# Cross-attention K and V products as one-pass three-term sums, scores in two double banks, softmax sums inverted through transfers

## Chip, cores and metric

The kernel runs on one core of a Trainium2 chip. The metric is the device time of one execution in microseconds (us); the figure for the kernel before is the median of three runs.

## The reference

One transformer block for 8 sequences of 256 tokens, 128 channels wide, with a context of 1601 tokens of 96 channels per sequence. All data are float32.

```python
attn_in  = adaln(x, cond, ...);  x = attn(attn_in, attn_in, sa_...) + x     # self: 256 keys
cross_in = adaln(x, cond, ...);  ctx_n = ln(context, ca_lnc_w, ca_lnc_b)
x = attn(cross_in, ctx_n, ca_...) + x                                       # cross: 1601 keys
h = gelu(adaln(x, cond, ...) @ ff_w1 + ff_b1);  x = h @ ff_w2 + ff_b2 + x

def attn(xq, ctx, wq, wkv, wo, bo):        # 16 heads of 64
    q = heads(xq @ wq);  k, v = split(ctx @ wkv)
    q, k = rope(q), rope(k)                # pairs (even, odd) turned by sine and cosine
    a = softmax(q k^T / 8);  return (a v) @ wo + bo
```

## The kernel before

Everything is kept transposed, channels on the partitions. Heads go in pairs of 2 x 64 = 128 rows. A step is one pair of heads of one sequence, so self-attention and cross-attention have 64 steps each. Each engine has an order written out by hand as a string of words (`CROSS` for cross-attention); a word such as `k1+1` is piece 1 of the K work, for the step one ahead, and `p5+-1` is piece 5 of the products with V, of the step behind. The engines run in their own order and meet only at semaphores, so what stands first in an engine's string and waits holds up all behind it. The ramp strings (`RAMP` and `ramp`) do the same for the change from self- to cross-attention, and the last strings for the end, where the feed-forward layer is worked in beside the last steps.

One cross step does this:

- K (`project_k`): four chunks of 512, 512, 512 and 65 keys. Each is a float32 matmul per head (two halves of the array's columns), into bank `PB[0]` or `PB[1]`. VectorE multiplies by the sine (`turn_k`, L1034, to SBUF `turned`); SyncE sends the rows swapped in pairs to `swapped`; VectorE multiplies the bank by the cosine in place (L1040) and adds `swapped` (L1047). ScalarE copies the bank to `KH`, which rounds it to fp32r, the one-pass format (L728), and VectorE writes the rest `KL = bank - KH` (L1055). Each of these VectorE instructions has one tensor in PSUM and one in SBUF.
- V (`project_v`, L1338): 13 tiles of 124 keys in four groups, float32, into the bank `XB`; ScalarE copies them out.
- Maxima (`max_scores`, L1357): one-pass products Q by K for the row maxima, in `MP`; VectorE reduces each (L1069), seven pieces.
- Scores (`scores`, L1376): 13 tiles in seven units, as four one-pass terms KH QH + KL QH + KH QL - maximum, in the one double bank `SP`; ScalarE takes the exponentials (L851), whose units 0 to 6 are called `e0` to `e6`, into four rotating buffers `P`.
- GpSimd adds the exponentials up (L701, L708), folds the sum (L713), and does the last two parts of Q's rotation (L685, L692). All its operands are in SBUF.
- Products with V (L1390) in `OB`, the sum over the keys (`sums`, L1399, 128x256 in `XB`), its reciprocal on VectorE (`invert`, L1080), the scaling (`divide`, L1086), the output product (L1409) and the addition to `xT` (`add`).

The orders of TensorE and VectorE before:

```python
"a4 k1+1 p2+-1 v3+-1 a5 n0 s4+-1 q+1 p3+-1 a6 s5+-1 p4+-1 v0 k2+1 n1 p5+-1 s6+-1 a0+1 v1 n2 s0 "
"a1+1 p6+-1 k3+1 v2 n3 s1 a2+1 sum+-1 k0+2 n4 s2 a3+1 p0 p1 o+-1 s3",
"am4 kc0+1 kt1+1 am5 qt+1 ka0+1 am6 qc+1 kl0+1 nm n0 kc1+1 ka1+1 kt2+1 kc2+1 n1 am0+1 kl1+1 ka2+1 am1+1 "
"kl2+1 kt3+1 am2+1 kc3+1 rc+-1 dv+-1 ka3+1 am3+1 kl3+1 ad+-1 kt0+2",
```

Of the kernel before, what the change touches and what calls it, by code (L numbers as in the profile page):

```python
# [21 lines left out]
SLOTS = 4  # L22

# [42 lines left out]
def block_kernel(nc, xT_in, cT_in, ctx_in, cols_in, cols96_in, ada_in, packs, w1_in, w2_in,  # L66
# [22 lines left out]
    CROSS = Cross("ca", DC, M, 124, 512,  # L89
# [11 lines left out]
    with ExitStack() as ctx:  # L101
# [5 lines left out]


        xT = sb("xT", [D, T])
        ainT = sb("ainT", [D, T])  # L110
        ctxT_all = sb("ctxT_all", [D, CTX])
# [14 lines left out]
        o_w = [sb(f"o_w{i}", [PAIR, D]) for i in range(PAIRS)]  # L126
# [6 lines left out]
        QH, QL = ([sb(f"{name}{i}", [PAIR, N], F32R) for i in range(UNROLL)] for name in ("QH", "QL"))  # L133
        MX = [sb(f"MX{i}", [PAIR, N], F32R) for i in range(2)]
        qturned, qswapped = ([sb(f"{name}{i}", [PAIR, N]) for i in range(2)] for name in ("qturned", "qswapped"))
        share = sb("share", [PAIR, D], F32R)
        Vb = [sb(f"V{i}", [D, len(CROSS.tiles), PAIR]) for i in range(2)]
        PR = [sb(f"P{i}", [D, 2, W]) for i in range(4)]
        psum_acc = sb("psum_acc", [D, 2, W])
        nmx = [sb(f"nmx{i}", [D, 2, 2], F32R) for i in range(2)]  # L140
        mxc = sb("mxc", [D, 2, 2, len(CROSS.chunks)])
        nmxc = [sb(f"nmxc{i}", [D, 2, 2], F32R) for i in range(2)]
        oraw = sb("oraw", [PAIR, N])
        oT = sb("oT", [PAIR, N])
        oraws = [sb(f"oraws{i}", [PAIR, N]) for i in range(2)]
        oTs = [sb(f"oTs{i}", [PAIR, N]) for i in range(PAIRS)]
        csq = [rope[:, i * CW:(i + 1) * CW].rearrange("p (t c) -> p t c", c=DC) for i in range(2)]
        ctree = sb("ctree", [D, 2 * CT, DC // 2])
# [3 lines left out]
        PB = [ctx.enter_context(nc.psum_tensor(f"PB{i}", [D, 512], F32)) for i in range(3)]  # L152
# [4 lines left out]

        SP, MP, KB, XB = S[0], S[1], PB[0:2], PB[2]

# [13 lines left out]
        s_cols = sem("context_columns_loaded")  # L173
        s_rope = sem("rotations_loaded")
        s_set = sem("constants_set")
        s_rows = sem("stack_rows_set")
# [4 lines left out]
        s_w1 = sem("ff_weights_loaded")  # L181
# [33 lines left out]
        class ContextNorm:  # L215

            def __init__(self):
                self.load = [sem(f"ctx_loaded{b}") for b in range(B)]
# [39 lines left out]
        class CrossSteps:  # L258

            def __init__(self, a):  # L260
                n = a.name
                self.w = [sem(f"{n}_weights_loaded{i}") for i in range(UNROLL)]
                self.wo = [sem(f"{n}_wo_loaded{i}") for i in range(UNROLL)]
# [3 lines left out]
                self.qswap = [sem(f"{n}_q_swapped{i}") for i in range(2)]  # L267
# [4 lines left out]
                self.kt = sem(n + "_k_turned")  # L272
                self.kc = sem(n + "_k_cosines")
# [16 lines left out]
                self.sum = sem(n + "_sum")  # L290
                self.inv = sem(n + "_sum_inverse")
# [9 lines left out]
        tree_ = ctree[:, :, :].rearrange("p a b -> p (a b)")  # L301
        LN2 = LayerNorm("ln2", 0, all_chunks[1:], [SP[:, 0], SP[:, 1]], OB, [MP[:, 0], MP[:, 1]],
                        [tree_[:, 0:LNC], tree_[:, LNC:2 * LNC], PR[3][:, 0]], QK)
        LN3 = LayerNorm("ln3", 1, all_chunks[:-1], KB, MP[:, 0, :], KB, [QK[0], QK[1], turned[2]],
# [30 lines left out]
        NM = 2 * NK - 1  # L335

# [17 lines left out]
        def q_free(eng, J):  # L354

            wait(eng, x.s, times(J, NU) - (UNROLL - 1) * NU)
# [27 lines left out]

        def halves(tile):
            return tile.rearrange("p (a n) -> p a n", n=N)
# [4 lines left out]
        def q_bank(J):  # L391

            return MP[:, 0, 0:N] if J == 0 else XB[:, 0:N]
# [37 lines left out]
        RAMP_DVE = {61: "kt0 kc0", 62: "ka0 kt1 kc1 qt0 qc0 kl0", 63: "ka1 kt2 kc2"}  # L431
        RAMP_ACT = {62: "kh0", 63: "qh0 kh1"}
# [42 lines left out]
        def _(sp):  # L475
# [4 lines left out]
            for dst, source in ((condT, cT_in), (ada, ada_in), (cols, cols_in), (ident, ident_in)):  # L480
                sp.dma_start(dst[:], source).then_inc(s_const, 16)
            def self_weights(J, _):
# [9 lines left out]
                for b in (0, 1) if J == 0 else (J,) if 2 <= J < B else ():  # L492
                    sp.dma_start(ctxT_all[:, TOK + b * CW:TOK + (b + 1) * CW], ctx_in[:, b * CW:(b + 1) * CW]
                                 ).then_inc(cx.load[b], 16)

            def self_swap(J, _):
# [4 lines left out]
                if J == B:  # L501
                    sp.dma_start(cols96[:], cols96_in).then_inc(s_cols, 16)
                if J == 2:
                    for pair in range(PAIRS):
                        sp.dma_start(o_w[pair][:, :], packs["sa"][2][pair]).then_inc(z.wo, 16)
                if ROPE <= J < ROPE + 4:
                    lo, hi = ((J - ROPE + i) * M // 2 for i in range(2))
                    sp.wait_ge(cx.tree, tree_end("var", B // 2 - 1, 2))
                    sp.dma_start(rope[:, lo:hi], rope_in[:, lo:hi]).then_inc(s_rope, 16)
# [39 lines left out]
            do = {"q": swap_q, "k": swap_k, "w": cross_weights_of, "wo": cross_out_weights_of}  # L549
            ramp = "w w+1 k0 k1 q k2 k3"  # L550
# [14 lines left out]
        def _(pool):  # L565
# [73 lines left out]
            def self_attention(do):  # L639
# [11 lines left out]

                def context_second(J, _):
# [23 lines left out]
                run_steps(SELF, in_order(SELF.pool, {"l": low_parts, "f": fold, "cc": context_ahead, "cp": context_first,  # L676
                                                     "cq": context_second}))

            def cross_words():

                def rotate_q(J, _):
                    i = J % 2
                    wait(pool, x.qc, times(J, 1) + 1)
                    wait(pool, x.qswap[i], J // 2 * 32 + 32)
                    pool.tensor_tensor(qrotb[i][:, :], qrotb[i][:, :], qswapped[i][:, :], ALU.add  # L685
                                       ).then_inc(x.qa, 1)

                def low_q(J, _):
                    r = J % UNROLL
# [5 lines left out]
                def accumulate(J, c):  # L695
# [26 lines left out]
            run_steps(a_, in_order(a_.pool, do, ahead(*RAMP_POOL[0].values(), *RAMP_POOL[1].values())))  # L722
# [3 lines left out]
        def _(act):  # L726
            def copy(out, in_):
                return act.activation(out, in_, ACT.Copy)  # L728

            def norm(ln, by=""):  # L730

                def square(k):
                    wait(act, ln.centred, k + 1)
                    wait(act, ln.var, k - 1)
                    act.activation(ln.sq[k % 2][:, :], ln.xc[k][:, :], ACT.Square).then_inc(ln.squared, 1)
# [18 lines left out]
            def self_attention(do):  # L754
# [48 lines left out]

                def context_out(J, _):
# [757 lines left out]
```

## Time and profile before

| | |
|---|---|
| median of 3 runs | 1933.77 us (1933.48 to 1937.64) |
| span of the profiled execution, first to last instruction | 1934.6 us |
| its own time outside the span | the profile gives none |
| busy: TensorE, VectorE, ScalarE, GpSimd | 98%, 82%, 49%, 65% |
| mean granted TensorE clock | 0.986 of full speed |

Matmuls are pipelined, so the busy time of one overlaps that of the next; what a group of them costs is read from its start to the start of the next group. A float32 matmul is shown as two records, an fp32r matmul as one. VectorE and GpSimd work one instruction at a time.

### The profile page before, as it was taken

To read this page: it belongs to the slowest core of one execution; us is meant where nothing else is said; L and a number is where in the kernel's file an instruction comes from. 1 tells how busy PE (TensorE), PEld (TensorE's weight loads), DVE (VectorE), ACT (ScalarE), POOL (GpSimd) and SP (SyncE) were. 2 spreads that over 40 slices of the span, in tenths; PEclk is the share of its full clock that TensorE was granted. 3 is DMA by queue.
4 is the path that set the end of the run, shared out by engine and by line. 5 is a ranking of instruction groups with operands and counts; after the bars stand their busy time and mean duration, and the time that the engine had idled before them with its cause. 6 is when DMAs were issued, how large, how long until landed. Compare 5 with 4: busy or idle time off the path is not lost.

```text
span 1934.6 us, 52084 instructions
## 1 busy us (share of the span) xinstructions
PE 1889.5 (98%) x19952; PEld 1289.2 (67%) x19952; DVE 1582.3 (82%) x2316; ACT 945.2 (49%) x1460; POOL 1266.3 (65%) x816
## 2 busy tenths in 40 slices
PE   7999999979999999999999999999999999999999
PEld 5666767745666666666666666666666666666664
DVE  4999999967888888888888888888888888888842
ACT  3555545533545444445554445455444445544444
POOL 4777756415776676677767677776776667667661
PEclk8999999978999999999999999999999999999999
DMA  5332233211111111111111111111111111111100
GB/s 176 117 88 86 81 112 88 73 33 48 53 54 53 55 51 53 59 55 54 54 51 55 52 58 57 51 56 51 55 50 56 57 54 56 51 53 52 53 29 23
DMA packets 147729, 119.07 MB, mean 62 GB/s; under 512 B 63392, under 2 KB 111648, under 8 KB 147488
## 3 DMA queue, kind: packets, MB, share of 16 engines
q1 hardware_dynamic: 110624, 115.46, 17.9%
q10 hardware_dynamic: 36864, 0.28, 1.0%
q8 instruction: 166, 2.72, 0.6%
q14 instruction: 75, 0.61, 0.1%
HBM read 36.71 MB, written 1.05 MB: 20 GB/s over the span
## 4 chain that ended last, share of the span: by engine, by line
PE 87%; POOL 4%; issue 3%; DVE 3%; DMA 1%; ACT 1%; SPq 0%; ACTq 0%; DVEq 0%; POOLq 0%
PE S L1376 24%; PE OB L1390 20%; PE PB L1338 10%; PE PB L1325 10%; PE S L1357 7%; PE PB L1399 2%; PE PB L1310 2%; PE S L1225 2%; PE PB L1409 1%; PE PB L1191 1%; PE OB L1253 1%; PE OB L1236 1%; DMA swapped<-turned 1%; POOL KL L667 1%; POOL psum_acc L674 1%
## 5 line engine op out<-in xcount | busy, mean ns | idle before, releaser
L708 POOL TENSOR_TENSOR psum_acc<-psum_acc,P 124x1024 f32<-124x1024 f32 (+1 forms) x320 | 689.8, 2156 | 216.9 <-ACT P L851 207.4
L851 ACT ACTIVATE P<-S 124x1024 f32<-124x1024 f32 (+1 forms) x448 | 431.3, 963 | 514.6 <-PE S L1376 513.9
L1069 DVE TENSOR_REDUCE mxc<-S 128x2 f32<-128x1024 f32 x384 | 470.0, 1224 | 94.9 <-PE S L1357 88.1
L1390 PE MATMUL OB<-P,V 124*64 124x256 f32 (+1 forms) x3328 | 437.3, 387 | 0.0
L1390 PEld LDWEIGHTS OB<-P,V 124*64 124x64 f32 (+1 forms) x3328 | 221.4, 137 | 188.7 <-issue 104.8
L701 POOL TENSOR_TENSOR psum_acc<-P 124x1024 f32<-124x1024 f32 x64 | 152.0, 2374 | 213.4 <-ACT P L851 213.4
L1376 PE MATMUL S<-QH,KH 64*124 64x256 f32 (+1 forms) x1664 | 271.8, 323 | 5.8 <-ACT P L851 5.8
L728 ACT ACTIVATE V<-PB 124x512 f32<-124x512 f32 (+1 forms) x320 | 157.2, 491 | 206.4 <-PE PB L1338 167.0
L1376 PEld LDWEIGHTS S<-QH,KH 64*124 64x124 f32 (+1 forms) x1664 | 154.0, 181 | 128.5 <-issue 104.7
L1376 PE MATMUL S<-QL,KH 64*124 64x256 f32 (+1 forms) x1664 | 235.2, 278 | 0.0
L1376 PE MATMUL S<-MX,share 64*124 64x256 f32 (+1 forms) x1664 | 235.0, 278 | 0.0
L1376 PE MATMUL S<-QH,KL 64*124 64x256 f32 (+1 forms) x1664 | 234.8, 278 | 0.0
L1338 PE MATMUL PB<-kv_w,ctxT_all 96*64 96x128 f32 (+2 forms) x3328 | 230.4, 276 | 0.4 <-DVE qrot L1024 0.4
L1325 PE MATMUL PB<-ctxT_all,kv_w 96*64 96x512 f32 (+1 forms) x1024 | 222.2, 512 | 0.1
L1338 PEld LDWEIGHTS PB<-kv_w,ctxT_all 96*64 96x64 f32 (+2 forms) x3328 | 187.4, 135 | 37.1 <-issue 17.7
L1034 DVE TENSOR_TENSOR turned<-PB,rope 128x512 f32<-128x512 f32 (+1 forms) x256 | 145.5, 568 | 74.4 <-PE PB L1325 74.4
L1357 PE MATMUL S<-KH,QH 64*128 64x512 f32 (+1 forms) x1024 | 189.5, 387 | 9.2 <-DVE mxc L1069 6.5
L728 ACT ACTIVATE KH<-PB 128x512 fp32r<-128x512 f32 (+1 forms) x256 | 128.6, 502 | 65.5 <-DVE PB L1047 61.9
L1047 DVE TENSOR_TENSOR PB<-PB,swapped 128x512 f32<-128x512 f32 (+1 forms) x256 | 147.8, 577 | 14.2 <-DMA swapped<-turned 11.8
L1376 PEld LDWEIGHTS S<-QH,KL 64*124 64x124 f32 (+1 forms) x1664 | 155.1, 183 | 3.0
L1376 PEld LDWEIGHTS S<-MX,share 64*124 64x124 f32 (+1 forms) x1664 | 155.2, 182 | 0.0
L1376 PEld LDWEIGHTS S<-QL,KH 64*124 64x124 f32 (+1 forms) x1664 | 154.4, 182 | 0.0
(159 smaller groups left out, 2844.8 us busy)
## 6 DMA issues: line engine op xcount, KB each, us to landing
swapped<-turned SPq DMA_DIRECT2D x512, 128.0 KB, 2.1
kv_w<-sa_kv_dram SPq DMA_DIRECT2D x64, 128.0 KB, 2.3
qswapped<-qturned SPq DMA_DIRECT2D x128, 64.0 KB, 1.9
kv_w<-ca_kv_dram SPq DMA_DIRECT2D x64, 96.0 KB, 2.2
ctxT_all<-ctx_dram SPq DMA_DIRECT2D x8, 624.0 KB, 4.4
q_w<-sa_wq_dram SPq DMA_DIRECT2D x64, 64.0 KB, 2.0
q_w<-ca_wq_dram SPq DMA_DIRECT2D x64, 64.0 KB, 2.0
o_w<-ca_wo_dram SPq DMA_DIRECT2D x64, 64.0 KB, 2.0
```

Of the source, the lines that this page charges most:

```text
L701: pool.tensor_tensor(acc, P_of(J, 0)[0:rows], P_of(J, 1)[0:rows], ALU.add).then_inc(x.acc, 2)
L708: pool.tensor_tensor(acc, acc, P_of(J, c)[0:rows, :, 0:w], ALU.add).then_inc(x.acc, 1)
L728: return act.activation(out, in_, ACT.Copy)
L851: act.activation(P_of(J, c)[0:rows, :, 0:w], SP[0:rows, :, 0:w], ACT.Exp, scale=SCALE).then_inc(x.e, 1)
L1034: dve.tensor_tensor(turned[c][:, 0:w], KB[c % 2][:, 0:w], rope[:, M + lo:M + lo + w], ALU.mult).then_inc(x.kt, 1)
L1047: dve.tensor_tensor(KB[c % 2][:, 0:w], KB[c % 2][:, 0:w], swapped[c][:, 0:w], ALU.add).then_inc(x.ka, 1)
L1069: dve.tensor_reduce(mxc[:, t, :, c:c + 1], MP[:, :, 0:w], AX.X, ALU.max).then_inc(x.am, 1)
L1325: ins = pe.matmul(KB[c % 2][half(h), 0:w], kv_w[J % UNROLL][0:DC, half(h)], ctxT_all[0:DC, at:at + w], start=True, stop=True)
L1338: ins = pe.matmul(XB[a:b, k * PAIR:(k + 1) * PAIR], ctxT_all[0:DC, lo + a:lo + b], kv_w[J % UNROLL][0:DC, PAIR:2 * PAIR], start=True, stop ...
L1357: ins = pe.matmul(MP[:, h, at:at + w], QH[J % UNROLL][half(h), t::2], KH[J % 2][half(h), lo:lo + w], start=True, stop=True)
L1376: ins = pe.matmul(SP[0:w, h, k * N:(k + 1) * N], keys[half(h)], queries[half(h), :], start=(n == 0), stop=(n == len(terms) - 1))
L1390: ins = pe.matmul(OB[half(h), 0:N], Vb[J % 2][0:w, t, half(h)], P_of(J, c)[0:w, h, k * N:(k + 1) * N], start=(t == 0), stop=(t == len(a_.t ...
```

## The change

K and V of the cross-attention are computed from operands split in a rounded part and a rest, as three one-pass terms: high by high, high by low, low by high. The context and the weights are split once each, by ScalarE (rounding copy) and GpSimd (rest), in the last self steps, the ramp, and, for later sequences, in the cross steps. K's matmuls take all 128 columns of the array; V's take the weights of two steps (256 columns) as the moving operand, so V is computed for two steps at once, in seven groups of two tiles.

```diff
 def project_k(J, c):
-    for h in range(2):
-        ins = pe.matmul(KB[c % 2][half(h), 0:w], kv_w[J % UNROLL][0:DC, half(h)],
-                        ctxT_all[0:DC, at:at + w], start=True, stop=True)
+    terms = ((1, high), (0, high), (0, low))
+    for n, (part, context) in enumerate(terms):
+        ins = pe.matmul(bank("k", c, J)[:, 0:w + o], wsplit[:, p, part * PAIR:(part + 1) * PAIR], context,
+                        start=(n == 0), stop=(n == len(terms) - 1))
 def project_v(J, k):
...
+        terms = ((low, 2), (high, 2), (high, 3))
+        for n, (context, part) in enumerate(terms):
+            ins = pe.matmul(bank("v", k, J)[0:w, i * 2 * PAIR:(i + 1) * 2 * PAIR], context,
+                            wsplit[:, p:p + 2, part * PAIR:(part + 1) * PAIR], ...)
```

The scores alternate between two double banks, `SP` and `PB`. The K and V products use the same banks in between, or `XB`; `bank_free` waits for the reader of whatever was in the bank last. So K leaves its bank at once: ScalarE copies it to SBUF (`read_k`, word `kq`), SyncE swaps its rows, and all of the rotation and the rest runs from SBUF to SBUF on VectorE:

```diff
+def read_k(J, c):
+    copy(turned[c][:, 0:a_.chunks[c][1]], k_bank(J, c)).then_inc(x.kq, 1)
 def rotate_k(J, c):
-    dve.tensor_tensor(KB[c % 2][:, 0:w], KB[c % 2][:, 0:w], swapped[c][:, 0:w], ALU.add)
+    raw, other = turned[c][:, 0:w], swapped[c][:, 0:w]
+    dve.tensor_tensor(other, other, rope[:, M + lo:M + lo + w], ALU.mult).then_inc(x.kc, 1)
+    dve.tensor_tensor(raw, raw, rope[:, lo:lo + w], ALU.mult).then_inc(x.kc, 1)
+    dve.tensor_tensor(raw, raw, other, ALU.subtract).then_inc(x.ka, 1)
 def low_k(J, c):
-    dve.tensor_tensor(KL[J % 2][:, lo:lo + w], KB[c % 2][:, 0:w], KH[...].bitcast(F32), ALU.subtract)
+    dve.tensor_tensor(KL[J % 2][:, lo:lo + w], turned[c][:, 0:w], KH[...].bitcast(F32), ALU.subtract)
```

The sum over the keys is copied to SBUF by ScalarE (`sc`), gathered as 128x4 by two transfers (`g`), inverted there by VectorE (`ri`), stored to DRAM by two transfers (`i`) and spread over the rows by two more (`b`); `divide` then reads two SBUF tensors:

```diff
 def invert(J, _):
-    dve.reciprocal(XB[:, 0:N], XB[:, 0:N])
+    wait(dve, x.spread, times(J, 96) + 32)
+    dve.reciprocal(stat[:, :, :], stat[:, :, :])
 def divide(J, _):
-    dve.tensor_tensor(oT[:, :], oraw[:, :], XB[:, 0:N], ALU.mult)
+    wait(dve, x.spread, times(J, 96) + 96)
+    dve.tensor_tensor(oT[:, :], oraw[:, :], sums_sb[:, :], ALU.mult)
```

All orders are new. TensorE's puts the scores in three groups (s0 s1, then s2 s3 s4, then s5 s6) and K two to three steps ahead:

```diff
-"a4 k1+1 p2+-1 v3+-1 a5 n0 s4+-1 q+1 p3+-1 a6 s5+-1 p4+-1 v0 k2+1 n1 p5+-1 s6+-1 a0+1 v1 n2 s0 "
-"a1+1 p6+-1 k3+1 v2 n3 s1 a2+1 sum+-1 k0+2 n4 s2 a3+1 p0 p1 o+-1 s3",
+"a2+1 s0 s1 a3+1 p5+-1 p6+-1 q+2 p0 p1 a4+1 s2 a5+1 s3 s4 a6+1 sum+-1 p2 o+-2 n0 p3 k1+2 v0 k2+2 a0+2 s5 s6  "
+"a1+2 p4 k3+2 n1 n2 v1 v2 k0+3 v3",                                                      # TensorE
+"dv+-2 ka3+1 kl1+1 am3+1 qt+2 am4+1 qc+2 am5+1 kl2+1 kl3+1 ka0+2 n0 am6+1 ad+-2 nm+1 ri+-1 kl0+2 am0+2 ka1+2  "
+"am1+2 ka2+2 n1 am2+2",                                                                  # VectorE
+"e0 e1 oe+-1 kh2+1 kh3+1 e2 e3 sc+-1 e4 kh0+2 n0 qh+2 kq1+2 ve0 mr+1 kq2+2 e5 e6 xh ve1 n1 kq3+2 kh1+2 n2  "
+"ve2 kq0+3 wh+5 ve3",                                                                    # ScalarE
+"c5+-1 cf+-1 c6+-1 ql+1 wl+4 xl+-2 c1 c2 qa+2 c3 c4",                                    # GpSimd
+"q+2 wo+-1 k0+2 g+-1 r+5 k1+2 k2+2 i+-1 k3+2 w+5 b+-1 n")                                # SyncE
```

GpSimd's last addition and the sum's matmul work in a buffer of their own (`folded`). Q has three slots for four. The maximum of the short chunk comes fifth of seven. The ramp and the end have new strings too; at the end the output of step 62 and the inverse of step 63 are worked in between the feed-forward products.

## Rows read from the trace of the kernel before

**Rows 1.** The page, busy time of each engine over the span.

```profile
PE 1889.5 (98%) x19952; PEld 1289.2 (67%) x19952; DVE 1582.3 (82%) x2316; ACT 945.2 (49%) x1460; POOL 1266.3 (65%) x816
```

**Rows 2.** Stretches: length, busy PE, PEld, DVE, ACT, POOL, then PEclk, DMA share, GB/s.

```profile
400.00:440.00 40.00, 33.00 (x186) 21.61 (x186) 18.85 (x32) 14.00 (x24) 2.79 (x3) 0.67 0.07 23
...
600.00:1000.00 400.00, 400.00 (x4456) 274.67 (x4452) 338.23 (x513) 198.11 (x300) 278.53 (x160) 1.00 0.17 54
...
1900.00:1935.00 35.00, 30.98 (x90) 13.73 (x90) 7.08 (x10) 15.62 (x24) 1.12 (x1) 0.98 0.08 30
...
1000.19:1022.83 22.64, 22.64 (x254) 15.54 (x252) 19.11 (x30) 11.30 (x17) 15.79 (x10) 1.00 0.18 59
```

**Rows 3.** What TensorE waited for in the whole span: us, times, longest.

```profile
PE S L1357 <- DVE mxc L1069: 6.5, 6, 2.3
PE S L1376 <- ACT P L851: 5.8, 3, 2.8
```

**Rows 4.** Timeline of TensorE, one cross step: start, us, line, records.

```profile
1000.19 0.51 PE L1357 MATMUL S<-KH,QH 64*128 64x512 f32 x2
1000.53 0.28 PE L1376 MATMUL S<-QH,KH 64*124 64x256 f32 x2
1000.65 0.28 PE L1376 MATMUL S<-QH,KL 64*124 64x256 f32 x2
...
1005.30 1.04 PE L1338 MATMUL PB<-kv_w,ctxT_all 96*64 96x128 f32 x16
1006.18 1.03 PE L1325 MATMUL PB<-ctxT_all,kv_w 96*64 96x512 f32 x4
1007.04 1.03 PE L1390 MATMUL OB<-P,V 124*64 124x256 f32 x8
...
1008.90 1.09 PE L1338 MATMUL PB<-kv_w,ctxT_all 96*64 96x128 f32 x16
1009.92 0.38 PE L1376 MATMUL S<-QH,KH 64*124 64x256 f32 x2
1010.14 0.28 PE L1376 MATMUL S<-QH,KL 64*124 64x256 f32 x2
1010.26 0.28 PE L1376 MATMUL S<-QL,KH 64*124 64x256 f32 x2
...
1014.72 1.03 PE L1325 MATMUL PB<-ctxT_all,kv_w 96*64 96x512 f32 x4
1015.68 0.38 PE L1376 MATMUL S<-QH,KH 64*124 64x256 f32 x2
```

**Rows 5.** Groups by line and shape: busy us, mean ns, idle before.

```profile
L1069 DVE TENSOR_REDUCE mxc<-S 128x2 f32<-128x1024 f32 x384 | 470.0, 1224 | 94.9 <-PE S L1357 88.1
L1034 DVE TENSOR_TENSOR turned<-PB,rope 128x512 f32<-128x512 f32 x192 | 131.6, 685 | 74.4 <-PE PB L1325 74.4
L1034 DVE TENSOR_TENSOR turned<-PB,rope 128x65 f32<-128x65 f32 x64 | 13.9, 217 | 0.0
L1080 DVE RECIPROCAL PB<-PB 128x256 f32<-128x256 f32 x64 | 112.4, 1756 | 12.3 <-PE PB L1399 12.3
L928 DVE RECIPROCAL lnrstd<-lnsd 128x4 f32<-128x4 f32 x3 | 0.5, 175 | 4.7 <-ACT lnsd L740 4.7
L1086 DVE TENSOR_TENSOR oT<-oraw,PB 128x256 f32<-128x256 f32 x64 | 26.9, 421 | 2.2
L708 POOL TENSOR_TENSOR psum_acc<-psum_acc,P 124x1024 f32<-124x1024 f32 x256 | 607.4, 2373 | 207.5 <-ACT P L851 207.1
L851 ACT ACTIVATE P<-S 124x1024 f32<-124x1024 f32 x384 | 393.1, 1024 | 427.7 <-PE S L1376 426.9 <-POOL psum_acc L708 0.5
L728 ACT ACTIVATE KH<-PB 128x512 fp32r<-128x512 f32 x192 | 114.1, 594 | 48.8 <-DVE PB L1047 48.5
```

**Rows 6.** DMA issues: KB each, median us from issue to landing.

```profile
swapped<-turned SPq DMA_DIRECT2D x512, 128.0 KB, 2.1
MX<-nmxc ACTq DMA_DIRECT2D x128, 1.0 KB, 2.0
```

More of the change, by code:

```diff
@@ L22 @@
 SLOTS = 4
+QSLOTS = 3
+LOADS = 2
+TOP = 229344
 class Stage:
@@ L217, in __init__ @@
             def __init__(self):
-                self.load = [sem(f"ctx_loaded{b}") for b in range(B)]
+                self.load = [sem(f"ctx_loaded{i}") for i in range(LOADS)]
                 self.tree = sem("ctx_tree")
@@ L262, in __init__ @@
                 self.w = [sem(f"{n}_weights_loaded{i}") for i in range(UNROLL)]
+                self.raw = [sem(f"{n}_kv_weights_loaded{i}") for i in range(UNROLL)]
+                self.wh = sem(n + "_kv_weights_high")
+                self.wl = sem(n + "_kv_weights_low")
+                self.xh = sem(n + "_context_high")
+                self.xl = sem(n + "_context_low")
                 self.wo = [sem(f"{n}_wo_loaded{i}") for i in range(UNROLL)]
@@ L266, in __init__ @@
                 self.qc = sem(n + "_q_cosines")
-                self.qswap = [sem(f"{n}_q_swapped{i}") for i in range(2)]
+                self.qswap = sem(n + "_q_swapped")
                 self.qa = sem(n + "_q_rotated")
@@ L290, in __init__ @@
                 self.sum = sem(n + "_sum")
+                self.sc = sem(n + "_sum_read")
+                self.spread = sem(n + "_sums_gathered_inverses_spread")
                 self.inv = sem(n + "_sum_inverse")
@@ L728, in copy, with high_weights, high_context @@
                 return act.activation(out, in_, ACT.Copy)
+            def high_weights(p, _):
+                if p < PAIRS:
+                    act.wait_ge(x.raw[p % UNROLL], p // UNROLL * 16 + 16)
+                    if p >= PAIRS // 2:
+                        wait(act, z.y, STEPS // 2)
+                    copy(split_of(p, 0), both_parts(raw_weights(p))).then_inc(x.wh, 1)
+            def high_context(b, k):
+                lo, w = a_.chunks[k]
+                act.wait_ge(cx.done, b * CG + k + 1)
+                if b > 1:
+                    wait(act, x.kp, (b - 1) * PAIRS * NK)
+                    wait(act, x.vp, (b - 1) * PAIRS // 2 * NU)
+                copy(ctxH[b % 2][:, lo:lo + w], ctxT_all[0:DC, b * M + lo:b * M + lo + w]).then_inc(x.xh, 1)
             def norm(ln, by=""):
@@ new lines, in project_k, with project_v @@
+                    terms = ((1, high), (0, high), (0, low))
+                    for n, (part, context) in enumerate(terms):
+                        ins = pe.matmul(bank("k", c, J)[:, 0:w + o], wsplit[:, p, part * PAIR:(part + 1) * PAIR], context,
+                                        start=(n == 0), stop=(n == len(terms) - 1))
+                    ins.then_inc(x.kp, 1)
+                def project_v(J, k):
+                    if v_group(J, k) is None:
+                        return
+                    m, g, n = v_group(J, k)
+                    b, p = batch(2 * m), 2 * m % PAIRS
+                    wait(pe, x.wl, min(2 * m + 1, PAIRS - 1) + 1)
+                    wait(pe, x.xl, b * NK + (sum(a_.tiles[a_.units[g][-1]]) - 1) // a_.chunks[0][1] + 1)
+                    bank_free("v", k, J)
+                    if J == -1:
+                        pe.wait_ge(LN2.unit, NLN - 1)
+                    for i, t in enumerate(a_.units[g]):
+                        lo, w = a_.tiles[t]
+                        high, low = ctxH[b % 2][:, lo:lo + w], ctxL[:, b * M + lo:b * M + lo + w]
+                        terms = ((low, 2), (high, 2), (high, 3))
+                        for n, (context, part) in enumerate(terms):
+                            ins = pe.matmul(bank("v", k, J)[0:w, i * 2 * PAIR:(i + 1) * 2 * PAIR], context,
+                                            wsplit[:, p:p + 2, part * PAIR:(part + 1) * PAIR],
+                                            start=(n == 0), stop=(n == len(terms) - 1))
@@ L1351, in max_scores @@
                         wait(pe, x.qc, 1)
-                    if u == 0 and J == 1:
-                        wait(pe, LN2.unit, NLN - 1)
-                    for t in range(2) if last else (u % 2,):
+                    for t in range(2) if last else (tile,):
                         for h in range(2):
                             at = t * N if last else 0
-                            ins = pe.matmul(MP[:, h, at:at + w], QH[J % UNROLL][half(h), t::2],
+                            ins = pe.matmul(MP[:, h, at:at + w], QH[J % QSLOTS][half(h), t::2],
                                             KH[J % 2][half(h), lo:lo + w], start=True, stop=True)
@@ L1375, in scores @@
                             for h in range(2):
-                                ins = pe.matmul(SP[0:w, h, k * N:(k + 1) * N], keys[half(h)], queries[half(h), :],
+                                ins = pe.matmul(slot(J, c)[0:w, h, k * N:(k + 1) * N], keys[half(h)], queries[half(h), :],
                                                 start=(n == 0), stop=(n == len(terms) - 1))
@@ L1406, in output @@
                     wait(pe, x.ot, times(J, 1) + 1)
-                    x_free(uses, readers, J, ("o", 0))
+                    bank_free("o", 0, J)
                     for h in range(2):
-                        ins = pe.matmul(XB[half(h), 0:N], o_w[r][:, half(h)], oT[:, :], start=True, stop=True)
+                        ins = pe.matmul(bank("o", 0, J)[half(h), 0:N], o_w[r][:, half(h)], oT[:, :], start=True, stop=True)
                     ins.then_inc(x.y, 1)
```

433 lines of the change are left out of this document (271 added, 162 removed), and 10 rows, old and new, of tables (CROSS, SELF).

## The prediction

> **What bounds the kernel now.** First the busy shares of the page: TensorE 98% [rows 1]. Then the stretches: in the cross steps, from 457 to about 1860 us, TensorE is busy all the time at the full clock, and one step of it, from one K/Q maximum group to its repeat, takes 22.64 us [rows 2]. In that step VectorE works 19.11 us, GpSimd 15.79 and ScalarE 11.30 [rows 2]. Then the waits: in the whole span TensorE waits some 6 us each for maxima and exponentials [rows 3]. So 62 of the 64 cross steps, about 1404 us, are TensorE's instruction stream and nothing else. A change is worth what it takes from this stream, as long as no other engine or chain becomes longer than the shorter step.
>
> **K and V products.** Read from start to start, a V group of four tiles takes 0.88 and 1.02 us, a K chunk of 512 keys 0.86 and 0.96 us [rows 4]. K has 1601/512 = 3.13 such chunks: 3.13 x 0.91 = 2.85 us a step. V has 13/4 = 3.25 such groups: 3.25 x 0.95 = 3.09. Together 5.94 us.
>
> After: a pair of one-pass matmuls of 256 columns, which lie on different rows of the array and run together, takes 0.12 us (1010.14 to 1010.26) [rows 4]. A K chunk is three matmuls of 512 columns on all the rows, 3 x 0.23 = 0.70 us plus a start of some 0.06, so 3.13 x 0.76 = 2.4 us a step. V is 39 matmuls of 256 columns in two steps, 19.5 a step, at 0.12: 2.35 us, with three to four starts 2.5. Together 4.9 us: a gain of 1.05 us a step. No row shows a one-pass matmul on 96 rows with 124 or 128 columns of weights. The bounds: nearly the rate of two rows-halves without any overhead, 0.107 us per 256 columns (0.12 less the 0.01 that the spacing may hold), gives 4.4 us and a gain of 1.5; a weight load that doesn't hide, at most the 0.28 us that one matmul record lasts [rows 4], would give 5.5 us for V alone and a loss of 2. I take 0.12, since in the scores two loads and two matmuls fit in that time.
>
> **Order of the score groups.** A score unit that follows a float32 group begins slowly: the second pair starts 0.22 us after the first (1009.92 to 1010.14), against 0.12 after a maximum group (1000.53 to 1000.65) [rows 4]. In the order before six of the seven units follow a float32 group. In the new one all seven follow a maximum group or another unit. That is 6 x 0.10 = 0.6 us a step. Bounds: 0 if the cost returns at other borders, 0.9 if the float32 groups gain at theirs. I take 0.5. The rest of TensorE's stream (13 tiles of scores and of products, maxima, Q, sum, output) is the same.
>
> **TensorE's step after**: 22.64 - 1.05 - 0.5 = 21.1 us.
>
> **VectorE.** The reciprocal falls from 1.76 to 0.18 us [rows 5]. Sine, cosine, join and rest keep their count, three of 512 and one of 65 columns each, at 0.69 and 0.22 us with one tensor in PSUM [rows 5]. So the step falls from 19.11 to 17.5 us, against 21.1: 3.6 us of slack. With both tensors in SBUF the instruction may be somewhat shorter or, if it has to share something, longer; this is the first rival. The reductions pace the maxima: 1.22 us [rows 5] plus a group of 0.34 [rows 4]; the new order has at least 1.4 us of scores between a long pair of them, except behind a4, which is now the short one.
>
> **ScalarE** gets the copies out of the K banks, 3 x 0.59 plus 0.2, the copy of the sum, 0.4, and V in pieces of 256 columns: 11.30 + 2.0 + 0.4 + 0.5 = 14.2 of 21.1 us. Busy time is no limit, its order may be: behind `mr+1`, which waits for the maximum of the next step, stand `kq2`, `e5` and `e6`, and for these TensorE's `k3`, `p4` and `s0`. From a6 to the end of s5 and s6 lie some 6.5 us of TensorE's work; `am6`, `ad` and `nm` need 1.9 of it. Hidden, and it costs up to 1 us a step if VectorE comes late by more than 3 us.
>
> **GpSimd** gets one more subtraction of context per two steps and, in all, eight of weights: 16 to 16.5 us of 21.1. The split of the first context falls in the last self steps, where GpSimd is idle, and ScalarE at half load: 0, at most 3 us.
>
> **Transfers.** The inverse takes three transfers one after another, 2.0 us each [rows 6], plus ScalarE's copy 0.4, and SyncE's queue. `sum` starts some 11 us into the step, the gather lands 3 us later; VectorE comes to `ri` about 2 us after a6, so it may stand 1 us there. SyncE waits at `b` for the store; behind it is only the next Q swap. The spread rows land 11 to 12 us after `sum`, and `dv+-2` is due at about 11.6. So VectorE stalls 1 to 2 us a step, out of 3.6 of slack. I take 0 to 0.2 us a step on TensorE for all new waits, +6 us in all; up to 1.5 a step if the slack is gone.
>
> **Ramp and end.** In the ramp TensorE has half clock for long (0.67 over 40 us) [rows 2]; the new string does more K and V before the first scores and fewer waits between: 0, bounds -15 and +20. At the end, `o0` waits for three transfers (7.5 us) with five feed-forward products, 4.3 us, in between: +3.
>
> **Sum**, against the span of 1934.6 us: 62 x (1.05 + 0.5) = -96, waits +6, end +3: 1847.6, and with the median 0.8 us below the span, 1847 us.
>
> **Rivals.** *First, the other side: VectorE and GpSimd get in each other's way at SBUF's read side.* Before, every large VectorE instruction had one tensor in PSUM, and GpSimd's ran beside it at a constant 2.37 us [rows 5]; no row shows a large VectorE instruction with two SBUF tensors, so none shows whether it can. After, 17 a step have two: 12 x 0.69 + 4 x 0.22 + 0.42 = 9.6 us [rows 5]. GpSimd reads two SBUF tensors in all its 15.8 us [rows 2]. If the two can't run at once, the step is at least 9.6 + 15.8 = 25.4 us; with the durations less their fixed part (0.15 us each for 27 instructions, from the 65- and 512-column forms) 21.4. In between, at 24 to 25, the decision falls to waits: in-order queues lose some again. It decides once the sum exceeds 21.1. 24.5 us gives 62 x 1.9 = +115, about 2050; the bounds are 1870 and 2140. For it: every VectorE form before avoids two SBUF tensors, and 9.6 + 15.8 is over the step. Against it: nothing in the trace, but if the ports share word by word only the lower end remains.
>
> The Trainium skill (SBUF — State Buffer, Who interferes with whom) states that a VectorE instruction with two SBUF inputs contends with a GpSimd instruction that reads SBUF, and that the one that comes second blocks until the first is done. By this rule the upper end holds, 25.4 us a step or more and about 2110 us. No row here can show it.
>
> *Second, new waits eat most of the gain.* The chains through `mr`, `ri` and `dv` and the banks shared by K, V and scores leave the step between 21.7 and 22.8 us. For it: the slack behind nm and dv is 1 to 3 us by the sums above, and a TensorE that idles can lose its clock, as in the ramp [rows 2]. Against it: VectorE's 17.5 us. 22.2 gives 62 x 0.45 = -28, with the end 1909; from 1880 to 1950.
>
> **Chances.** Forecast (1815 to 1880) 0.44; first rival 0.33; second 0.23, of which 0.13 is faster, 0.04 the same and 0.06 slower. A time within 0.2% (1930 to 1938) counts as the same, about what a measurement of this kernel can tell. Faster 0.57, same 0.04, slower 0.39. The range runs from 1810 to 2090: 0.03 lies below and half of the first rival above. The likeliest case's own range is 1815 to 1880.
>
> **What would show it.** A step of 21 us in TensorE's timeline with K chunks at 0.70 to 0.76 us and V groups of six matmuls at 0.72 to 0.8, second score pairs at 0.12 throughout: the forecast. GpSimd's 1024-column additions still at 2.37 us and VectorE's 512-column forms at 0.69 or less: the first rival is wrong; additions of 3 us, or VectorE forms of 1 to 3 us, and TensorE waiting for maxima or exponentials: it is right. Waits of TensorE for `P` with both engines' durations unchanged: the second. My forecast is wrong if the step is above 21.7 us.

## The result, and the profile after

The changed kernel takes 2563.81 us (median of 4 runs, 2557.99 to 2566.91) against 1934.62 us (4 runs): a ratio of 1.325, 95% interval 1.3225 to 1.3276. Slower by a third; the prediction was 1847 and its range ended at 2090. The profiled execution has a span of 2557.8 us. In the fences, the page's busy times, as in [rows 1]; then stretches with the columns of [rows 2], the third of them one cross step between two of Q's matmuls.

```profile
PE 2002.2 (78%) x17616; PEld 1449.0 (57%) x17616; DVE 2195.7 (86%) x2316; ACT 1072.2 (42%) x2011; POOL 1423.5 (56%) x856
```

```profile
400.00:440.00 40.00, 29.52 (x122) 22.17 (x121) 20.39 (x34) 15.06 (x32) 0.98 (x2) 0.63 0.06 21
600.00:1000.00 400.00, 302.11 (x2639) 222.82 (x2640) 355.07 (x360) 161.50 (x315) 221.57 (x116) 0.86 0.13 39
1499.99:1532.62 32.63, 24.52 (x215) 17.68 (x213) 28.83 (x30) 12.68 (x25) 17.70 (x10) 0.84 0.13 39
```

This step went from 22.64 to 32.6 us. The mean of the cross steps, read from one combination of the row maxima (VectorE's `nm`, one a step) to the next, is 32.45 us, and 62 x 9.8 = 608 is nearly the whole loss of 623 between the spans. TensorE no longer fills the step; VectorE does, with 28.8 us in the same 30 instructions, where the forecast had 17.5. Next, the groups of instructions by line and shape (columns of [rows 5]), VectorE's and GpSimd's:

```profile
L1219 DVE TENSOR_TENSOR turned<-turned,rope 128x512 f32<-128x512 f32 x192 | 334.5, 1742 | 0.0
L1218 DVE TENSOR_TENSOR swapped<-swapped,rope 128x512 f32<-128x512 f32 x192 | 322.1, 1678 | 7.5 <-DMA swapped<-turned 7.3
L1228 DVE TENSOR_TENSOR KL<-turned,KH 128x512 fp32r<-128x512 f32 x192 | 252.6, 1316 | 10.6 <-ACT KH L867 10.2 <-issue 0.2
L1221 DVE TENSOR_TENSOR turned<-turned,swapped 128x512 f32<-128x512 f32 x192 | 207.3, 1080 | 6.6
L1259 DVE TENSOR_TENSOR oraws<-oraws,qturned 128x256 f32<-128x256 f32 x64 | 138.3, 2161 | 52.8 <-DMA qturned<-inverses_dram 52.4
L1242 DVE TENSOR_REDUCE mxc<-S 128x2 f32<-128x1024 f32 x384 | 468.6, 1220 | 148.1 <-PE S L1555 147.9
...
L840 POOL TENSOR_TENSOR psum_acc<-psum_acc,P 124x1024 f32<-124x1024 f32 x256 | 634.6, 2479 | 840.6 <-ACT P L1028 831.1
L850 POOL TENSOR_TENSOR folded<-psum_acc 124x512 f32<-124x512 f32 x64 | 103.2, 1612 | 5.0
L827 POOL TENSOR_TENSOR QL<-qrot,QH 128x256 fp32r<-128x256 f32 x64 | 74.8, 1168 | 1.1 <-ACT QH L867 1.1
```

Every 512-column VectorE form with two SBUF tensors has grown, from 0.69 to 1.1 to 1.7 us, and the division from 0.42 to 2.16; the reduction from PSUM keeps its 1.22 [rows 5]. Of the 65-column forms only the rest has grown (0.22 to 0.79). GpSimd's long additions pay less, 2.48 for 2.37 us; its short instructions pay more: the fold 1.61 for 1.28, the rest of Q 1.17 for 0.73. The timelines of both engines (start, us, line) show how:

```profile
1502.44 2.87 DVE L1218 TENSOR_TENSOR swapped<-swapped,rope 128x512 f32<-128x512 f32 x1
1505.23 2.82 DVE L1219 TENSOR_TENSOR turned<-turned,rope 128x512 f32<-128x512 f32 x1
1508.09 0.69 DVE L1221 TENSOR_TENSOR turned<-turned,swapped 128x512 f32<-128x512 f32 x1
1508.70 1.22 DVE L1242 TENSOR_REDUCE mxc<-S 128x2 f32<-128x1024 f32 x1
1509.83 0.41 DVE L1127 TENSOR_TENSOR xT<-xT,XB 128x256 f32<-128x256 f32 x1
```

```profile
1502.40 5.11 POOL L840 TENSOR_TENSOR psum_acc<-psum_acc,P 124x1024 f32<-124x1024 f32 x2
```

GpSimd's first addition starts 0.04 us before VectorE's, which then lasts one addition and its own 0.6; the second does the same, and ends 0.55 us (one short instruction) after GpSimd's pair, at 1508.05 against 1507.51. Once GpSimd stands still, the next form takes 0.69. What TensorE pays for it, in its timeline and in the waits of the whole span (us, times, longest; compare [rows 3]; the first of these is ScalarE's, whose copy of K to `KH` TensorE's maxima need):

```profile
1510.39 1.19 PE L1517 MATMUL XB<-ctxH,wsplit 96*128 96x512 f32 x2 [5.98 <-DVE xT L1127]
```

```profile
ACT KH L867 <- DVE turned L1221: 412.4, 68, 6.8
...
PE XB L1517 <- DVE xT L1127: 300.3, 52, 6.0
...
PE S L1555 <- DVE mxc L1242: 89.2, 71, 5.1
...
PE OB L1588 <- ACT oraws L867: 57.1, 59, 1.9
```

The K product of chunk 2 needs `XB`, which `ad` (L1127) must have read; `ad` stands in VectorE's order behind `kl2 kl3 ka0`, five instructions with two SBUF tensors.

### The profile page after: what moved, and what is told of

Read it like the earlier page. It is cut to its first block, busy times and chain, and to the rows that moved or that the text cites. A ratio compares the mean times of both kernels' runs of the same rounds, so it can differ in the third digit from the quotient of the medians.

```text
span 2557.8 us, 48174 instructions
## 1 busy us (share of the span) xinstructions
PE 2002.2 (78%) x17616; PEld 1449.0 (57%) x17616; DVE 2195.7 (86%) x2316; ACT 1072.2 (42%) x2011; POOL 1423.5 (56%) x856
## 4 chain that ended last, share of the span: by engine, by line
DVE 38%; PE 35%; issue 9%; DMA 8%; SPq 5%; ACT 3%; POOL 2%; ACTq 0%; DVEq 0%; POOLq 0%
DVE KL L1228 8%; DVE turned L1219 8%; PE OB L1588 8%; DVE swapped L1218 8%; DMA qturned<-inverses_dram 5%; DVE oraws L1259 5%; PE XB L1517 4%; DVE mxc L1242 4%; PE S L1555 4%; PE S L1574 4%; PE PB L1574 4%; SPq L633 2%; DMA swapped<-turned 2%; PE S L1399 1%; DVE turned L1221 1%
## 5 line engine op out<-in xcount | busy, mean ns | idle before, releaser
L840 POOL TENSOR_TENSOR psum_acc<-psum_acc,P 124x1024 f32<-124x1024 f32 x256 | 634.6, 2479 | 840.6 <-ACT P L1028 831.1
L1517 PE MATMUL XB<-ctxH,wsplit 96*128 96x512 f32 x248 | 98.2, 487 | 348.7 <-DVE xT L1127 300.3
L1219 DVE TENSOR_TENSOR turned<-turned,rope 128x512 f32<-128x512 f32 (+1 forms) x256 | 348.3, 1360 | 0.0
L1218 DVE TENSOR_TENSOR swapped<-swapped,rope 128x512 f32<-128x512 f32 (+1 forms) x256 | 335.9, 1312 | 8.4 <-DMA swapped<-turned 8.2
L1588 PE MATMUL OB<-P,V 124*64 124x256 f32 (+1 forms) x2236 | 298.8, 400 | 39.5 <-ACT oraws L867 39.4
L1228 DVE TENSOR_TENSOR KL<-turned,KH 128x512 fp32r<-128x512 f32 (+1 forms) x256 | 298.5, 1185 | 10.6 <-ACT KH L867 10.2
L1028 ACT ACTIVATE P<-PB 124x1024 f32<-124x1024 f32 (+1 forms) x224 | 215.7, 963 | 182.2 <-PE PB L1574 176.2
L1028 ACT ACTIVATE P<-S 124x1024 f32<-124x1024 f32 (+1 forms) x224 | 215.8, 963 | 176.6 <-PE S L1574 174.4
L1221 DVE TENSOR_TENSOR turned<-turned,swapped 128x512 f32<-128x512 f32 (+1 forms) x256 | 221.9, 867 | 8.8
L1259 DVE TENSOR_TENSOR oraws<-oraws,qturned 128x256 f32<-128x256 f32 x64 | 138.3, 2161 | 52.8 <-DMA qturned<-inverses_dram 52.4
L1574 PE MATMUL PB<-QH,KH 64*124 64x256 f32 (+1 forms) x832 | 142.4, 328 | 7.9 <-DMA MX<-nmxc 3.2
```

Source lines behind the costliest of these rows:

```text
L1028: act.activation(P_of(J, c)[0:rows, :, 0:w], slot(J, c)[0:rows, :, 0:w], ACT.Exp, scale=SCALE).then_inc(x.e, 1)
L1218: dve.tensor_tensor(other, other, rope[:, M + lo:M + lo + w], ALU.mult).then_inc(x.kc, 1)
L1219: dve.tensor_tensor(raw, raw, rope[:, lo:lo + w], ALU.mult).then_inc(x.kc, 1)
L1221: dve.tensor_tensor(raw, raw, other, ALU.subtract).then_inc(x.ka, 1)
L1228: dve.tensor_tensor(KL[J % 2][:, lo:lo + w], turned[c][:, 0:w], KH[J % 2][:, lo:lo + w].bitcast(F32), ALU.subtract).then_inc(x.kl, 1)
L1259: dve.tensor_tensor(oT[:, :], oraw[:, :], sums_sb[:, :], ALU.mult).then_inc(x.ot, 1)
```

## The experiments

Theory: the two engines exclude each other at SBUF, whole instruction by whole instruction, and VectorE's in-order queue turns that into TensorE's waits. Rivals: the new waits themselves (transfers, banks, orders), or slower one-pass products.

**Take GpSimd's load away (a1, a4).** L1218 to L1259 are as in the change.

```diff
-acc = psum_acc[0:rows, :, 0:w];  ... P_of(J, c)[0:rows, :, 0:w]
+acc = psum_acc[0:rows, :, 0:8];  ... P_of(J, c)[0:rows, :, 0:8]        # a4: 0:256
```

> The changed kernel with GpSimd's additions of the exponentials cut to 8 of their columns (the sums are left wrong; every instruction, wait and order stays). Theory A, VectorE's instructions with two SBUF tensors and GpSimd's block each other: the 512-column K instructions of VectorE fall from means of 1.1 to 1.7 us to 0.7, the step from 32.6 to 21 to 22 us, the time to 1840 to 1920 us. Theory B, the step is long through the new chains of waits (transfers of the inverse, shared banks, in-order queues) and VectorE's durations are long for another reason, such as ScalarE's and the DMAs' traffic in SBUF: durations stay over 1 us and the time over 2400 us.

> The changed kernel with GpSimd's additions cut to half of their columns (256 of 512 per head; the sums are left wrong), 1.28 us each for 2.37. Theory A: what VectorE is held up falls about by half, the step to 26 to 28 us, the time to 2150 to 2300 us. Theory B: over 2400 us.

a1: 2055.69 us (1.0631 [1.06, 1.0662]); a4: 2263.62 (1.1706 [1.1672, 1.174]). With additions of 0.35, 1.39 and 2.48 us the time is 2056, 2264 and 2564: some 200 and 275 us per microsecond of one. Where TensorE or the transfers set the time, it would not follow an engine that idles over 40% of it. a4 is as expected; a1 lies 136 us above the 1840 to 1920 expected. It still has the folds, at 1.60 us, and Q's rest, at 1.17; VectorE's 512-column K forms take 0.71 to 0.97 us in it, so some contention is left, and a2 shows a second cause.

**Take VectorE's second tensor away (a2).** K's rotation, its rest and the division read one SBUF tensor each, through a reduction over groups of one element; the rotation, the rest and the scaling are left out, GpSimd does all its work.

```diff
-dve.tensor_tensor(other, other, rope[:, M + lo:M + lo + w], ALU.mult)
+dve.tensor_reduce(other, other.rearrange("p (n a) -> p n a", a=1), AX.X, ALU.max)
```

> The changed kernel with VectorE's SBUF-to-SBUF instructions of K and the scaling by the inverse replaced by instructions of the same width with one SBUF tensor (a reduction over an axis of length 1; rotation, rest and scaling are left out). GpSimd keeps all its additions. Theory A: about 0.6 to 0.7 us each, GpSimd's additions at 2.37 us, the time 1840 to 1920 us. Theory B, or GpSimd's additions being late by themselves: over 2300 us.

2003.09 us (1.0359 [1.03, 1.0418]). Its groups:

```profile
L1213 DVE TENSOR_REDUCE turned<-turned 128x512 f32<-128x512 f32 x192 | 129.8, 676 | 0.0
...
L840 POOL TENSOR_TENSOR psum_acc<-psum_acc,P 124x1024 f32<-124x1024 f32 x256 | 609.8, 2382 | 361.5 <-ACT P L1028 344.7 <-DMA qswapped<-qturned 7.0
```

Same count, same bytes written, same GpSimd, and both engines are back at their durations of before. 561 of the 623 us are gone. But 2003 is above the 1840 to 1920 expected, and the kernel is still slower than before: its steps take 23.47 us in the mean, against 22.64 before and the forecast's 21.1. So there is a second cause.

**Two SBUF tensors in the kernel before (a3).** The rest of K is taken from `turned` instead of the bank.

```diff
-dve.tensor_tensor(KL[...], KB[c % 2][:, 0:w], KH[...].bitcast(F32), ALU.subtract)
+dve.tensor_tensor(KL[...], turned[c][:, 0:w], KH[...].bitcast(F32), ALU.subtract)
```

> The kernel before with a single operand changed: the rest of K (KL) is taken from the SBUF tile turned in place of the PSUM bank, so that one VectorE form of four has two SBUF tensors (the values of KL are wrong). Theory A: its mean goes from 0.68 us to about 1.5 us (GpSimd is busy 70% of a step, and half an addition is 1.2 us), 2.5 us a step inside VectorE's 3.5 us of slack: 1935 to 2000 us. Theory B: it stays at 0.68 us and the time at 1934 us.

1946.08 us (1.0072 [1.0044, 1.01]). Its groups, then VectorE's timeline and GpSimd's:

```profile
L1055 DVE TENSOR_TENSOR KL<-turned,KH 128x512 fp32r<-128x512 f32 x192 | 224.6, 1170 | 1.5 <-ACT KH L728 0.3
L1047 DVE TENSOR_TENSOR PB<-PB,swapped 128x512 f32<-128x512 f32 x192 | 133.0, 693 | 12.3 <-DMA swapped<-turned 10.1
```

```profile
998.69 1.47 DVE L1055 TENSOR_TENSOR KL<-turned,KH 128x65 fp32r<-128x65 f32 x1
...
1012.49 0.68 DVE L1055 TENSOR_TENSOR KL<-turned,KH 128x512 fp32r<-128x512 f32 x1
```

```profile
997.72 2.36 POOL L708 TENSOR_TENSOR psum_acc<-psum_acc,P 124x1024 f32<-124x1024 f32 x1 [0.40 <-ACT P L851]
...
1012.54 1.77 POOL L708 TENSOR_TENSOR psum_acc<-psum_acc,P 113x512 f32<-113x512 f32 x1
```

One more SBUF operand is enough: this form alone grows, its neighbour with a bank does not. The first pair shows VectorE second: 65 columns, worth 0.22 us, end with GpSimd's addition at 1000.1. The second pair shows GpSimd second: VectorE keeps 0.68, and the 512-column addition takes 1.77 us (this one averages 1.49 in the span). It is symmetric, and holds for whole instructions, not word by word. The Trainium skill (SBUF — State Buffer, Who interferes with whom) says just this, that the second blocks until the first is done; both pairs agree with it. The form's mean is 1.17 us, less than the 1.5 expected, and in this kernel it costs 13 us: VectorE had slack.

**Without the transfers (b4, and b2 with a2's instructions).** VectorE inverts the 128x256 sum in SBUF; `g`, `i` and `b` are gone.

```diff
-wait(dve, x.spread, times(J, 96) + 32);  dve.reciprocal(stat[:, :, :], stat[:, :, :])
+wait(dve, x.sc, times(J, 1) + 1);        dve.reciprocal(sums_sb[:, :], sums_sb[:, :])
```

> The changed kernel with the sum inverted by VectorE as 128x256 in SBUF, without transfers; contention as in the changed kernel. If VectorE sets the step: 1.6 us more of it a step, less the 52 us for which it waits for the spread rows: 2590 to 2640 us. If the transfers are in the loop instead: 2450 to 2530 us.

> The one-input kernel (no contention, rotation left out) with the sum inverted at once by VectorE as 128x256 in SBUF, without the six transfers. If TensorE's waits for the copy of the output (51 us) and the 6.4 us at the end come from the transfers: 1935 to 1985 us, in spite of 1.6 us more of VectorE a step. Rival: VectorE's longer step moves the waits to the maxima, and the time stays at 2000 us or above.

b4: 2540.89 (1.3135 [1.3096, 1.3174]), between the two cases, 23 us less than the change though VectorE's reciprocal takes 1.6 us more a step. b2: 1908.15 (0.9865 [0.9842, 0.9888]), below both cases expected, 95 us less than a2 (whose two executions lie 9 us apart) and the only run under the kernel before; it leaves out the rotation, the rest and the scaling as a2 does. This is the second cause: without contention the chain of transfers costs 95 us where 6 were forecast for all new waits. In a2 VectorE waits for it, and TensorE behind it, though VectorE is busy only 73% of the stretch from 600 to 1000 us. In b2 the mean step is 22.15 us. First a2's wait, then that stretch of b2, with the columns of [rows 2]:

```profile
DVE oraws L1213 <- DMA qturned<-inverses_dram: 162.3, 63, 7.0
```

```profile
600.00:1000.00 400.00, 394.67 (x3887) 292.66 (x3887) 336.26 (x524) 237.66 (x458) 292.56 (x171) 1.00 0.15 51
```

**Only VectorE's order (b3).** `ad` ahead of the rests of K, and with b4's edit (c2).

```diff
-qc+2 am5+1 kl2+1 kl3+1 ka0+2 n0 am6+1 ad+-2 nm+1 ri+-1 kl0+2
+qc+2 am5+1 ka0+2 n0 am6+1 ad+-2 nm+1 kl2+1 kl3+1 ri+-1 kl0+2
```

> The changed kernel with two words of VectorE's order moved: the rests kl2+1 and kl3+1 now stand behind the maxima am6, the addition ad+-2 and nm. If the step is set by what VectorE is held up in all (it is busy 88% of a step), the 348 us that TensorE waits for the addition go elsewhere and the time falls by 0 to 100 us, 2460 to 2565. Rival: the loss is the position of the addition behind the blocked instructions, and the time falls below 2350 us.

> The changed kernel with both edits: the rests kl2 and kl3 behind ad and nm in VectorE's order (alone 139 us less), and the sum inverted by VectorE as 128x256 in SBUF without transfers (alone 23 us less). If VectorE and GpSimd blocking each other sets the time and the order only shows where it falls, the two add to 2564 - 139 - 23 = 2400. If with a good order the step is bound by VectorE's and GpSimd's added port time, the 1.6 us longer reciprocal is paid in full (62 x 1.6 = 100 us) against the transfers' waits, and the time is 2450 to 2520.

b3: 2424.62 (1.2534 [1.2498, 1.2569]), 139 us less by moving two words: more than the 0 to 100 of the first case, less than the rival's. So neither case holds alone: the position of the addition counts, and so does what VectorE is held up in all. One of its waits, 300.3 us in the change:

```profile
PE XB L1517 <- DVE xT L1127: 191.5, 52, 5.7
```

c2: 2452.68 (1.2678 [1.2644, 1.2712]; 2441 to 2467), above the 2400 of two gains that add, at the low end of the other case: 28 us more than b3. The gain of the transfers' removal turned into a loss, which fits VectorE's added time counting once the order is better. How the 100 us of its longer reciprocals and the waits saved balance was not separated.

**The products alone (b1).** The kernel before, with K and V from one-pass terms (V for two steps at once), but with the rotation in PSUM, the inverse in PSUM, one double bank of scores and the orders of before, with V's groups regrouped:

```diff
-"... p3+-1 a6 s5+-1 p4+-1 v0 k2+1 n1 p5+-1 s6+-1 a0+1 v1 n2 s0 a1+1 p6+-1 k3+1 v2 n3 ..."
+"... p3+-1 a6 s5+-1 p4+-1 v2+-1 k2+1 n1 p5+-1 s6+-1 a0+1 v3+-1 n2 s0 a1+1 p6+-1 k3+1 v0 n3 ..."
```

> The kernel before with only the products of the change: V as one-pass terms for two steps at once (seven groups of two tiles in the one bank XB) and K as one-pass terms in its two banks; the scores stay in one double bank, K is rotated in PSUM as before, the sum is inverted in PSUM, orders and ramp as before. K costs the same (0.82 us a chunk against 0.91 before, plus 0.36 for the short chunk), V 19.5 x 0.12 plus 3.5 starts of 0.1 = 2.7 us a step against 3.1. Theory A with TensorE's stream as the bound: 22.1 to 22.3 us a step, 1895 to 1920 us. Rival: the seven uses of XB in two steps for four before, each behind ScalarE's copy, cost waits that eat it: 1930 to 1980 us.

1980.13 us (1.0234 [1.0213, 1.0254]), the upper end of the rival; the forecast's 1.05 us a step would have made it 1870. TensorE's timeline, then two lines of the kernel before:

```profile
1005.85 1.08 PE L1584 MATMUL OB<-P,tree_room 124*64 124x256 f32 x8
1006.87 0.38 PE L1530 MATMUL XB<-wsplit,ctxL 96*124 96x256 f32 x1
1007.09 0.40 PE L1530 MATMUL XB<-wsplit,ctxH 96*124 96x256 f32 x2
1007.33 0.28 PE L1530 MATMUL XB<-wsplit,ctxL 96*124 96x256 f32 x1
1007.44 0.40 PE L1530 MATMUL XB<-wsplit,ctxH 96*124 96x256 f32 x2
1007.68 0.63 PE L1511 MATMUL PB<-ctxH,wsplit 96*128 96x512 f32 x2
1008.15 0.39 PE L1511 MATMUL PB<-ctxL,wsplit 96*128 96x512 f32 x1
1008.47 1.08 PE L1584 MATMUL OB<-P,o_room 124*64 124x256 f32 x8
```

```profile
1021.65 1.03 PE L1390 MATMUL OB<-P,V 124*64 124x256 f32 x8
1022.51 0.39 PE L1338 MATMUL PB<-kv_w,ctxT_all 96*64 96x128 f32 x4
```

The rates are as forecast: 0.12 us per 256 columns, so 0.23 for the weights' two halves on one context, and 0.70 for a K chunk plus 0.09 to the next float32 group. But V's group of two tiles takes 0.81 us here, 0.10 of it after P·V, and P·V itself, a float32 group, takes 1.02 us between one-pass groups (1005.85 to 1006.87) against 0.86 between float32 groups (1021.65 to 1022.51). The whole of TensorE's step, from start to start by line, marked waits taken off (mean of the steps from 600 to 1400 us):

| us a step | K | V | scores | P·V | maxima | Q, sum, output | waits | step |
|---|---|---|---|---|---|---|---|---|
| before | 2.84 | 3.20 | 6.90 | 5.96 | 2.25 | 1.50 | 0.00 | 22.64 |
| b1 | 2.92 | 2.85 | 6.88 | 6.41 | 2.27 | 1.60 | 0.27 | 23.20 |
| b2 | 2.73 | 2.45 | 6.77 | 6.02 | 2.50 | 1.56 | 0.12 | 22.15 |

In b1 K and V together gain 0.27 us, a quarter of the forecast's, the float32 groups (P·V, Q, sum, output) take 0.55 more, which fits their new borders, and new waits cost 0.27. 62 x 0.56 = 35 of the 43 us between the spans; most of the rest is in the first two steps.

**TensorE's order of scores, in the kernel before (c1).** Five of the seven score groups change places with the maximum group behind them, so that they no longer follow a float32 group; the other two follow a maximum group already.

```diff
-"... n1 p5+-1 s6+-1 a0+1 v1 n2 s0 a1+1 p6+-1 k3+1 v2 n3 s1 a2+1 sum+-1 k0+2 n4 s2 a3+1 p0 p1 o+-1 s3"
+"... n1 p5+-1 a0+1 s6+-1 v1 n2 a1+1 s0 p6+-1 k3+1 v2 n3 a2+1 s1 sum+-1 k0+2 n4 a3+1 s2 p0 p1 o+-1 a4+1 s3"
```

> The kernel before with only TensorE's order changed: in five places of a step the score group now follows the maximum group that stood behind it, so that it no longer follows a float32 group. My forecast's term (0.10 us for each score unit that no longer follows a float32 group) gives 5 x 0.10 x 62 = 31 us less, 1904. The rival: the maxima are now pushed two to three at a time closer to each other, and VectorE's 1.22 us reductions pace them, or the float32 group that now follows a score group starts slower by the same amount; then 1930 or more.

1955.1 us (1.0124 [1.0109, 1.0139], 4 runs against 7 of before, 1932.27): 1.2% slower, clear of the interval, and not the 1904 of the forecast's term. TensorE's timeline:

```profile
1000.96 0.51 PE L1357 MATMUL S<-KH,QH 64*128 64x512 f32 x2
1001.31 0.28 PE L1376 MATMUL S<-QH,KH 64*124 64x256 f32 x2
1001.43 0.28 PE L1376 MATMUL S<-QH,KL 64*124 64x256 f32 x2
...
1002.13 0.28 PE L1376 MATMUL S<-MX,share 64*124 64x256 f32 x2
1002.34 1.95 PE L1390 MATMUL OB<-P,V 124*64 124x256 f32 x16
...
1021.21 0.51 PE L1357 MATMUL S<-KH,QH 64*128 64x512 f32 x2 [0.29 <-DVE mxc L1069]
```

The second pair now starts 0.12 us after the first, as the forecast had it. But maximum and scores together last 1.38 us (1000.96 to 1002.34); in the kernel before, scores and maximum lasted 1.37 (1009.92 [rows 4] to 1011.29). The cost sits at the border between float32 and one-pass work, whoever stands there; swapping neighbours moves it. The mean step is 23.0 us; 0.21 of the 0.37 more are marked waits, most of them the rival's, for the maxima.

## Why the prediction was wrong

- **The failed step is VectorE's: "So the step falls from 19.11 to 17.5 us, against 21.1: 3.6 us of slack".** It was 28.8 us. The durations of 0.69 were read from forms with one tensor in PSUM and carried to forms with two in SBUF. The doubt was named and became a rival with 0.33; a1, a2, a3 and a4 show this rival right in kind.
- **The rival's price was too low.** It had 24 to 25 us a step, 2050; the step was 32.6. The sum 9.6 + 15.8 = 25.4, which I called "at least", is a floor for the two ports; I then took a value below it, though the text said that in-order queues lose some again. VectorE waits a whole addition to do 0.6 us of work, over and over (17.5 became 28.8), and TensorE gets its maxima, `XB` and `oraws` late. GpSimd's 840 us of idleness before L840 say that the ports were not used all the time. b3's 139 us from two words are a part of that loss.
- **The transfers**, 0 to 0.2 us a step, 6 us in all: wrong. Without contention they are worth 95 us (b2 against a2): 1.3 us a step (23.47 against 22.15) and 6 at the end. The text had 1.5 us a step as the price where the slack is gone; but in a2 VectorE has over 6 us of idleness a step. TensorE waits there 51.3 us for `oraws`, which ScalarE may fill again only behind the division, 17.3 for maxima and 14.1 for `XB`, together 83, just 62 x 1.3. A stall at one place of an in-order queue reached TensorE, though the queue was idle for longer than that elsewhere. With contention they cost 23 us net of the longer reciprocal (b4).
- **TensorE's stream of 21.1 us**: a third of the gain came. b2 has no contention and no transfers, and its mean step is 22.15 us: 0.49 less than before, where 1.55 were forecast. By the table of b1, K and V gave 0.86 of the 1.05 (the second of two V groups behind one another 0.71 us, a K chunk 0.79 against 0.76). The scores gave 0.13 of the 0.5: that term was wrong as a reason (c1), and its count was too, as five of the seven units, not six, followed a float32 group before. "The rest of TensorE's stream is the same" was wrong by 0.37, of which 0.25 stand behind the maxima, short unmarked gaps among them, and waits took 0.12. What can be saved is the number of borders between float32 and one-pass groups: between b1 and b2, where K and V stand next to scores and to each other, K, V and P·V together fall by 0.98 us.
- **Ramp and end**: forecast 0 and +3. The first `nm` starts at 422.6 us before, 423.3 in the change and 422.9 in b2; the interval behind it is 38.9, 46.8 and 38.5 us; from the last `nm` to the end are 70.4, 80.0 and 71.3 us, in a2 77.0. So ramp and end without contention and transfers cost 1 us, the transfers add 6 at the end (in a2 TensorE stands 6.4 us before the last output product), and the change loses 8 more in the ramp and 3 more at the end.
- **The books**, on the spans: contention 2557.8 - 1996.5 = +561 (a2); transfers 1996.5 - 1905.4 = +91 (b2); the rest, 1905.4 - 1934.6 = -29, is TensorE's shorter stream, 62 x 0.49 = 30, and 1 of ramp and end.
- **The clock** fell to 0.86 in the cross steps. In a2, b2 and before it is 1.00 there (600 to 1000 us), with the same kinds of matmuls; so I take the fall for a consequence of TensorE's waits, which makes the loss larger. By how much was not measured.

## What to carry to other kernels

Before moving a VectorE operand from PSUM to SBUF, ask what GpSimd does then: with a second SBUF tensor each instruction may cost a whole instruction of GpSimd, and the sum of both engines' times is the floor and not the estimate, as the in-order queue behind it spreads the delay to every bank and buffer it frees. Slack in the mean doesn't cover a stall at one place of such a queue either (a2). And read a step as the mean of many: single steps of b2 lie up to 1 us, of a2 up to 2 us from theirs. Test it with one form in the old kernel first (a3): one line, and the durations tell. And count the borders between float32 and one-pass groups, not what stands beside what; a swap of neighbours moves a cost (c1), fewer borders lower it (b2 against b1).

## What the runs showed of the hardware

- VectorE with two SBUF tensors against GpSimd with two: the second to start waits for the first's end, both ways (1.47 instead of 0.22 us; 1.77 instead of 1.29). With one SBUF tensor and PSUM, or one SBUF tensor alone, neither is touched (0.69; 0.676 and 2.38).
- In the change GpSimd's 1024-column additions grow by 5%, its fold by 26% and its two instructions for Q by 60%; VectorE's 512-column forms grow by 57 to 154% and the division fivefold.
- Each border between float32 and one-pass matmuls costs about 0.1 us (the second pair of scores behind one starts 0.22 us after the first instead of 0.12; in c1 the last pair ahead of one takes 0.21; in b1 P·V with borders on both sides takes 1.02 us instead of 0.86), at the full clock.
- One-pass matmuls on 96 rows: 0.12 us for 256 columns on 124 weights' columns, 0.235 for 512 on 128; the weight loads hide.
